# Audio tower, first attention: projections, turned blocks and output projection placed inside and behind the first pass

## What is computed

```python
h = _L0_tok_ref(x, L0_tok_W, L0_tok_b)
h = h + _L0_attn_ref(_layernorm(h, axis=-1), L0_attn_Wq, L0_attn_Wk, L0_attn_Wv, L0_attn_Wo, L0_attn_bo)
h = h + _L0_ffn_ref(_layernorm(h, axis=-1), L0_ffn_gate_w, L0_ffn_gate_b, L0_ffn_w1, L0_ffn_b1, L0_ffn_w2, L0_ffn_b2)
...
attn = jnp.einsum('bhqd,bhkd->bhqk', q, k)
causal_mask = jnp.triu(jnp.ones((T, T), dtype=bool), k=1)
attn = jnp.where(causal_mask, -jnp.inf, attn)
attn = jax.nn.softmax(attn, axis=-1)
out = jnp.einsum('bhqk,bhkd->bhqd', attn, v)
```

## Time and profile before

| what | value |
|---|---|
| median of 3 runs | 817.16 us (812.59 to 818.09) |
| the profiled execution's own time | 813.25 us |
| its span, first to last instruction | 811.4 us |
| mean granted TensorE clock | 0.948 of 2.4 GHz |
| TensorE busy | 715.2 us, 88% |
| VectorE busy | 446.1 us, 55% |
| ScalarE busy | 353.0 us, 44% |

### The profile page before, as it was taken

The page is one execution under the profiler, slowest core; times in us unless marked ns, Lnnn a source line. Parts: engine busy times, 40 slices in busy tenths (PEclk is TensorE's granted clock), DMA queues, the critical chain, the costliest instruction groups (busy, mean ns, idle before and its releaser), DMA issues.

```text
span 811.4 us, 16105 instructions
## 1 busy us (share of the span) xinstructions
PE 715.2 (88%) x5664; PEld 581.6 (72%) x5664; DVE 446.1 (55%) x1117; ACT 353.0 (44%) x602; POOL 137.8 (17%) x174
## 2 busy tenths in 40 slices
PE   6587998898898999999999999998899999998732
PEld 4466677676676999999999999996566665664411
DVE  4546766766655443244322232232768888866685
ACT  2242353253253322112222122222998998988351
POOL 2010111311311221000000100101552323211013
PEclk9799999999999999999999999999999999999755
DMA  6979474474365665655555655571874447650002
GB/s 178 210 97 246 55 92 66 66 91 69 55 86 182 220 216 176 240 188 190 160 182 189 211 194 159 194 195 46 111 116 76 72 64 105 79 70 9 1 26 78
DMA packets 70711, 102.67 MB, mean 127 GB/s; under 512 B 8160, under 2 KB 58472, under 8 KB 70512
## 3 DMA queue, kind: packets, MB, share of 16 engines
q1 hardware_dynamic: 67504, 93.34, 51.2%
q0 software_dynamic: 3136, 8.40, 4.1%
HBM read 63.88 MB, written 12.58 MB: 94 GB/s over the span
## 4 chain that ended last, share of the span: by engine, by line
PE 62%; DVE 17%; ACT 7%; issue 5%; DMA 5%; POOL 2%; SPq 1%; POOLq 0%; DVEq 0%; ACTq 0%
PE psum L1936 17%; PE psum L1987 17%; DVE arena L1285 8%; PE psum L1640 4%; DVE arena L1151 4%; PE psum L1648 3%; DMA arena<-arena 3%; PE psum L1879 3%; PE psum L1885 2%; PE psum L1703 2%; PE psum L1894 2%; PE psum L1682 1%; ACT arena L836 1%; ACT arena L835 1%; PE psum L1665 1%
## 5 line engine op out<-in xcount | busy, mean ns | idle before, releaser
L1936 PEld LDWEIGHTS psum<-arena 128*128 128x128 f32 x1248 | 144.9, 192 | 2.1 <-issue 0.2
L1936 PE MATMUL psum<-arena 128*128 128x128 f32 x1248 | 146.1, 275 | 0.1
L1987 PE MATMUL psum<-arena 128*128 x624 | 141.4, 380 | 1.2 <-DVE arena L1431 0.8
L865 ACT ACTIVATE arena<-psum,arena 128x128 f32<-128x128 f32 x156 | 44.5, 368 | 191.8 <-PE psum L1936 113.4
L1987 PEld LDWEIGHTS psum<-arena 128*128 128x128 f32 x624 | 115.5, 190 | 15.9 <-issue 1.8
L1413 DVE TENSOR_SCALAR arena<-psum,arena 128x128 f32<-128x128 f32 x156 | 43.9, 344 | 81.7 <-PE psum L1936 63.5
L1894 PE MATMUL psum<-arena 96*128 96x256 bf16 x512 | 75.8, 276 | 10.1 <-ACT arena L835 6.1
L1285 DVE TENSOR_TENSOR arena<-arena 128x1024 f32<-128x1024 f32 x64 | 80.0, 1316 | 4.9 <-ACT arena L835 2.6
L1894 PEld LDWEIGHTS psum<-arena 96*128 96x128 bf16 x512 | 45.0, 98 | 45.5 <-ACT arena L836 14.3
L702 POOL DMA_INDIRECT w0T<-yg,pos x32 | 37.4, 1169 | 223.2 <-DMA yg<-arena 176.8
L1431 DVE TENSOR_TENSOR arena<-psum,arena 128x256 f32<-128x256 f32 x39 | 16.6, 425 | 96.6 <-PE psum L1987 96.6
(11 more groups left out here) (288 smaller groups left out, 1192.9 us busy)
## 6 DMA issues: line engine op xcount, KB each, us to landing
arena<-in_L_ffn_w_dram SPq DMA_DIRECT2D x47, 1024.0 KB, 11.5
arena<-arena SPq DMA_DIRECT2D x192, 128.0 KB, 5.9
arena<-xg SPq DMA_DIRECT2D x39, 128.0 KB
yg<-arena SPq DMA_DIRECT2D x39, 128.0 KB, 1.7
out_dram<-arena SPq DMA_DIRECT2D x8, 256.0 KB, 2.1
xg<-zeros SPq DMA_DIRECT2D x9, 128.0 KB, 2.6
arena<-in_x_dram SPq DMA_DIRECT2D x8, 128.0 KB, 7.2
arena<-in_L_ffn_b_dram SPq DMA_DIRECT2D x1, 1024.0 KB, 12.2
```

What stands on the lines that cost most here:

```text
L865: ins = act.activation(hidT[:, v, c, :], psum[:, 2 * v, c * P:(c + 1) * P], ACT.Relu, bias=b1c[:, v, c:c + 1])
L1936: mm = pe.matmul(psum[:, 2 * v + c // HALF, (c % HALF) * P:(c % HALF + 1) * P], w1b[:, i % W1_BUFS, d, c * P:(c + 1) * P], xtT[:, v, d, :] ...
L1987: mm = pe.matmul(y_bank, hidT[:, u, c, :], w2s[:, one(e), c, :].rearrange("p o n -> p (o n)"), start=(c == 0), stop=(c == HC - 1))
```

## The change

No arithmetic changes; the order and two places do.

- The first pass uses two areas (banks 0 to 3), each pair waiting for the reduce two pairs back. Banks 4 and 5 are free during it.
- TensorE makes single pairs by `maxima(p)`. The next batch's input is turned behind pair 0, the router's input behind 1, the attention's last output behind 2; the router's logits (now in bank 6) stand behind pair 4, the k projection behind 5. Behind pair 7 follow the turned normalised output, q, the turned maxima (now in bank 4), the output projection and v; then the second pass, with nothing of the output projection in it.
- VectorE's reciprocals stand behind its third reduce, the gate logits and the normalised output behind its sixth. Behind the maxima it takes k's remainder, then q's. The residual add and statistics of batch b-1 come ahead of the token add of batch b+2, q's last part behind that, both normalisations ahead of the ranks.
- ScalarE sends the row of maxima on its own queue and casts k's high half first, during the first pass. The middle parts are cast ahead of the copy of v.
- SyncE sends k's parts ahead of q's and no longer waits for the maxima.
- The small products of the expert plan move from bank 7 to bank 6.

The core of the diff (what is only moved away in TensorE's program is in the listing above; `weights(p)` calls `shifted_scores`, `values(g)` calls `weigh_values`, `turned_input` is the turn behind `xh_done`):

```diff
         area = [psum[:, 0:2, :], psum[:, 2:4, :]]
-        area3 = [*area, psum[:, 4:6, :]]
...
-        early_cand = psum[:, 7, P:P + EARLY_TILES]
...
+        early_cand = psum[:, 6, P:P + EARLY_TILES]
+        turned_max = psum[:, 4, :].bitcast(BF16)
...
-                        sp.wait_ge(S["mT_done"], b + 1)
-                        sp.dma_start(stackq[SHIFT_ROW:SHIFT_ROW + 1, u], mT[0:HEADS, :]).then_inc(S["mrow"], 16)
                     if stages(b + 1, 0, LAST):
                         v = 1 - u
+                        spread(b + 1, v, 0, 1, S["kh_done"], S["stk_k"])
...
-                        spread(b + 1, v, 0, 1, S["kh_done"], S["stk_k"])
+                        spread(b + 1, v, 1, 1, S["km_done"], S["stk_k"])
                         spread(b + 1, v, 1, 0, S["qm_done"], S["stk_q"])
-                        spread(b + 1, v, 1, 1, S["km_done"], S["stk_k"])
+                        spread(b + 1, v, 2, 1, S["kl_done"], S["stk_k"])
                         spread(b + 1, v, 2, 0, S["ql_done"], S["stk_q"])
-                        spread(b + 1, v, 2, 1, S["kl_done"], S["stk_k"])
 
                 batches(sp, iteration, B)
...
                         act.copy(x2T.rearrange("p c t -> p (c t)"), misc[0]).then_inc(S["xt2_done"], 1)
+                    if stages(b + 1, 0, LAST):
+                        act.wait_ge(S["k_mm"], b + 2)
+                        wait(act, S["stk_k"], 16 * SLOTS6 * (b + 1))
+                        act.copy(qkp[1][:, 0].rearrange("p c t -> p (c t)"), misc[1]).then_inc(S["kh_done"], 1)
+                    if stages(b - 1, 0, LAST):
+                        act.wait_ge(S["ot2_mm"], b)
+                        wait(act, S["wo_mm"], b - 1)
+                        act.copy(oT.rearrange("p c t -> p (c t)"), turned[:, 1, :]).then_inc(S["oT_done"], 1)
                     if stages(b, 0, LAST):
                         act.wait_ge(S["mT_mm"], b + 1)
                         wait(act, S["mrow"], 16 * b)
-                        act.copy(mT[0:HEADS, :], misc[0].bitcast(BF16)[0:HEADS, 0:T]).then_inc(S["mT_done"], 1)
+                        act.copy(mT[0:HEADS, :], turned_max[0:HEADS, 0:T]).then_inc(S["mT_done"], 1)
+                        act.wait_ge(S["mT_done"], b + 1)
+                        act.dma_start(stackq[SHIFT_ROW:SHIFT_ROW + 1, u], mT[0:HEADS, :]).then_inc(S["mrow"], 16)
...
+                        act.wait_ge(S["kr_done"], b + 2)
+                        act.copy(qkp[1][:, 1], qkr[1]).then_inc(S["km_done"], 1)
+                        act.wait_ge(S["qr_done"], b + 2)
+                        act.copy(qkp[0][:, 1], qkr[0]).then_inc(S["qm_done"], 1)
...
+                    def maxima(p):
+                        if stages(b, 0, LAST):
+                            if p == 0:
+                                wait(dve, S["mneg_done"], 2 * b)
+                            dve.wait_ge(S["sn_mm"], PAIRS * b + p + 1)
+                            dve.tensor_reduce(mx[:, 2 * p:2 * p + 2, :],
+                                              area[p % 2][:, :, 0:3 * P].rearrange("p i (n k) -> p i n k", k=P),
+                                              AX, ALU.max).then_inc(S["mx_done"], 1)
+
                     if isinstance(b, int) and b == 0:
                         candidates()
+                    for p in range(3):
+                        maxima(p)
+                    if stages(b - 1, 0, LAST):
+                        dve.wait_ge(S["ot1_mm"], b)
+                        wait(dve, S["on_done"], QT * (b - 1))
+                        for q in range(QT):
+                            dve.reciprocal(rr[:, q, :], o1[:, q, :, DH]).then_inc(S["rr_done"], 1)
+                    for p in range(3, 6):
+                        maxima(p)
+                    if stages(b - 2, 0, LAST):
+                        gate_logits(b - 2, misc[0])
+                    if stages(b - 1, 0, LAST):
+                        wait(dve, S["ot2_mm"], b - 1)
+                        for q in range(QT):
+                            dve.wait_ge(S["rr_done"], QT * (b - 1) + q + 1)
...
+                    for p in range(6, PAIRS):
+                        maxima(p)
...
+                    if stages(b + 1, 0, LAST):
+                        wait(dve, S["km_done"], b + 1)
+                        wait(dve, S["kl_done"], b + 1)
+                        split_rest(b + 1, 1, S["kh_done"], S["kr_done"])
+                        wait(dve, S["qm_done"], b + 1)
+                        wait(dve, S["ql_done"], b + 1)
+                        split_rest(b + 1, 0, S["qh_done"], S["qr_done"])
...
-                        split_last(b + 1, 0, S["qm_done"], S["ql_done"])
                         split_last(b + 1, 1, S["km_done"], S["kl_done"])
+                    if stages(b - 1, 0, LAST):
+                        dve.wait_ge(S["wo_mm"], b)
+                        dve.wait_ge(S["hbo_done"], b)
+                        v = h[:, bass.ds((b - 1) * QT, QT), :]
+                        dve.tensor_tensor(v, misc[1].rearrange("p (q d) -> p q d", q=QT), v, ALU.add).then_inc(S["h1_done"], 1)
+                        dve.wait_ge(S["h1_done"], b)
+                        wait(dve, S["xn_done"], QT * (b - 1))
+                        statistics(b - 1, 1, S["stat2"], S["mv2"])
...
+                def scores_for_max(b, u, p):
...
+                    if p < 2:
+                        wait(pe, S["exp_done"], PAIRS * b - 1 + p)
+                    else:
+                        pe.wait_ge(S["mx_done"], PAIRS * b + p - 1)
+                    for i in range(2):
+                        hd = 2 * p + i
+                        dst = area[p % 2][:, i, :]
...
+                    maxima(0)
+                    if not (isinstance(b, int) and b == 0):
+                        turned_input()
+                    maxima(1)
                     if stages(b - 2, 0, LAST):
...
                         turn(misc[0], lambda q, c: x2h[:, u, q, c * P:(c + 1) * P], S["xt2_mm"])
+                    maxima(2)
                     if stages(b - 1, 0, LAST):
                         pe.wait_ge(S["oa_done"], b)
...
+                    maxima(3)
+                    maxima(4)
+                    if stages(b - 2, 0, LAST):
+                        pe.wait_ge(S["xt2_done"], b - 1)
...
+                        mm.then_inc(S["lg_mm"], 1)
+                    maxima(5)
+                    if stages(b + 1, 0, LAST):
+                        pe.wait_ge(S["xT_done"], b + 2)
...
+                        project_rows(misc[1], 1, S["k_mm"])
+                    maxima(6)
+                    maxima(7)
+                    if stages(b - 1, 0, LAST):
+                        pe.wait_ge(S["on_done"], QT * b)
+                        turn(turned[:, 1, :], lambda q, c: onat[:, q, c * P:(c + 1) * P], S["ot2_mm"])
+                    if stages(b + 1, 0, LAST):
+                        wait(pe, S["gl_done"], b - 1)
+                        project_rows(misc[0], 0, S["q_mm"])
...
                     if stages(b, 0, LAST):
...
                         for q in range(QT):
-                            mm = pe.transpose(misc[0].bitcast(BF16)[0:HEADS, q * P:(q + 1) * P], mneg[:, q, :], identb[:])
+                            mm = pe.transpose(turned_max[0:HEADS, q * P:(q + 1) * P], mneg[:, q, :], identb[:])
                         mm.then_inc(S["mT_mm"], 1)
...
+                    if stages(b - 1, 0, LAST):
+                        pe.wait_ge(S["oT_done"], b)
+                        upto(pe, "kr_done", b + 1)
+                        project_tokens(misc[1], oT, lambda c: w0T[:, 3, c, :], S["wo_mm"])
                     if stages(b + 1, 0, LAST):
...
                         wait(pe, S["mT_done"], b + 1)
...
                         project_tokens(turned[:, 0, :], xT, lambda c: w0T[:, 2, c, :], S["v_mm"])
...
                     if stages(b, 0, LAST):
                         pe.wait_ge(S["mrow"], 16 * (b + 1))
-                        shifted_scores(b, u, 0)
-                        shifted_scores(b, u, 1)
+                    weights(0)
+                    weights(1)
```

204 lines of the change are left out of this document (78 added, 126 removed).

## The result

The changed kernel takes 794.06 us (median of 4 runs, 793.29 to 795.36) beside 817.09 for the kernel before (812.59 to 818.09) on the same chip: a ratio of 0.973, interval 0.969 to 0.977. It is 23 us faster, against 32 forecast (817 to 785); the time lies inside the range. Between the two profiled executions the spans fell from 811.4 to 793.6 us, 17.8 less against 29.6 forecast.

What follows compares the result with a forecast made beforehand. No engine was taken as full: they take turns in eight attention rounds. Shorter rounds, VectorE last, total 202.8 against 232.4 us; 813.25 less 29.6 is 783.7, with drift 785, range 776 to 799.

Steps and rivals of the forecast that it cites:

- The full round, 26.3: Rounds 4 to 7: VectorE's 20.9 busy, 1.9 small gaps, 2.1 before reduces and 1.4 new wait; gain 3.5 on 29.8 us.
- the new wait: VectorE, between k's remainder and q's, waits for ScalarE's cast of q's high half behind the row's issue: 1.4 us.
- The first pass, forecast at about 10: Score products and reduces with TensorE's moved work inside: about 10 us for TensorE and VectorE, against 9.6 before.
- VectorE is the last: In a full round VectorE's 26.3 us outlasts TensorE's 25.6 and the transfers' 24.4 to 25, so it sets the length.
- The third chain: Stack transfers of q and k: complete 24.4 to 25 us into a full round, under 1.5 to spare, the next bound.
- The 2.1 before reduces: VectorE's waits before first-pass reduces, 2.1 us a round, kept because a reduce started late beside GpSimd's add.
- The sum of 25.1 a round: Full-round length if, by the port rule, a reduce reading only PSUM does not stand still: 25.1 us.
- Two areas, 0.3 a round: First pass: each pair waits for the reduce two back, costing 0 to 1.5 us a round, taken as 0.3.
- Round 2, 24.5: Second round: 24.3 us by the 3.5 gain; transfers behind four weight megabytes make it 24.5, against 27.8 before.
- the rival I called slower: Row of maxima lands only with stack transfers, 11.6 us; 7.0 in each of eight rounds, time 840; chance 0.04.
- the forecast of the last round, 23.5: Round 8, without next projections: output projection's 1.9 and 0.6 of order go, 23.5 us against 26.0 before.
- 202.8 forecast: All eight rounds of the first attention together: 202.8 us against 232.4 before, 29.6 less.

Runs made afterwards that it cites:

- eleventh experiment: Changed kernel with round 2's weights later, eight unread last-round products, q's last part earlier, and scaling and first scan filling VectorE's wait for q: 793.7 us, ratio 0.971.
- fourth: Changed kernel with q's last part made on VectorE right behind k's last part, ahead of both additions and their statistics: 793.8 us, ratio 0.970.
- fifth: Changed kernel with the output projection back in the second pass and the earlier order of additions, norms and ranks: 795.6 us beside 804.7, ratio 0.987.
- sixth: Changed kernel with k's projection directly ahead of q's, behind the first pass's last pair, instead of between pairs 5 and 6: 793.6 us beside 804.7, ratio 0.987.
- last experiment: Changed kernel with GpSimd's four scatters held until the last reduce of the first pass: 797.2 us, ratio 0.978.
- third experiment: Kernel before with two bank areas instead of three in the first pass, nothing else changed: 813.8 us, ratio 0.997.
- the one execution that stands in for the changed kernel: Changed kernel with GpSimd's output-bias addition cut from 2x256 to 2x8 columns, other columns' bias left out, executed once: 784.3 us beside 804.7.
- tenth: Changed kernel with round 2's 4 MB of expert weights behind its stack transfers and eight unread products added in the last round: 790.9 us, ratio 0.971.
- seventh experiment: Kernel before with only the row of maxima sent by ScalarE instead of SyncE: 804.6 us, ratio 0.998.

## Why the prediction was right, and where it was too good

**The full round, 26.3: right in its length.** Measured 26.7 and 26.5 at full clock on this chip. Its terms: VectorE busy 20.7 to 20.9 (20.9 forecast), the new wait 1.6 to 1.8 (1.4), the waits before reduces and the reciprocal 0.50 + 0.41 + 1.04 + 0.54 = 2.5 (2.1 for reduces). TensorE is busy 24.7, not 25.6. The first pass, forecast at about 10, takes 10.8 from the first reduce to the end of the last (140.06 to 150.84), and the second pass, forecast at about 9.2, 9.8 (155.64 to 165.39). Round 3, 25.6 forecast for want of scatters, took 25.3.

**"VectorE is the last": only half right.** The third chain, of which I had written that it was the next bound, runs beside it. Filling VectorE's wait for q (eleventh experiment) and making q's last part earlier (fourth) bought nothing. What did move the next start is an earlier cast of q's high half: by 1.1 us with the row from SyncE, for a round shorter by 0.9, and by 1.2 on the second chip, where the reduces have no gaps (12.8 us up to the cast and 12.4 behind it, 13.96 and 12.49 in the changed kernel). Rounds 4 to 6 of the kernels with the changed order (the fifth and sixth experiments aside, which alter it) take 12.3 to 12.9 from there, except the last, which takes 13.4 to 13.6 as VectorE holds TensorE up. In these 12 us TensorE and the transfers are full together; no run parts the two. So VectorE counts up to the cast, where it alternates with TensorE, and behind it only once it is late, as in the last experiment.

**Where the gain came from.** At the same clock of 1.00 on this chip a round 4 with two areas alone (third experiment) is 12.6 up to the cast and 16.3 behind it, the changed kernel's 14.0 and 12.7. So the first part did not get shorter but longer, by 1.3, and the second shorter by 3.5, as TensorE's work there fell from 15.6 to 12.1 us: k's projection and two turns of blocks now stand ahead of the cast, while the output projection stays behind it for the most part, at another place. By the experiments k's place is worth about 2.0 us a full round and the output projection's 1.0 with the cover that it gives the row, both against the one execution that stands in for the changed kernel. These do not add up to the whole, as each fills waits that the other leaves.

**The 2.1 before reduces: right size, wrong cause.** I read the gap of 1.21 beside GpSimd's addition as held by it, against the Trainium skill's rule that the prediction cites. The addition stands beside reduces with 0.18 of gap, or none, in the kernels with k beside q and with the row alone moved. The reduces beside it agree with the Trainium skill ("SBUF — State Buffer", Who interferes with whom), by which a reduce of PSUM is not held by the port it shares with GpSimd. The gaps belong to the rounds with scatters and leave the pass with them. The sum of 25.1 a round that I had worked out by that rule is near what the second chip shows, 25.2, in part by luck, since VectorE's chain alone does not set the round.

**Two areas, 0.3 a round: nothing in the kernel before.** The ratio there is 0.997 (0.994 to 1.001); in the changed kernel, where products stand between the pairs, it was not measured by itself.

**Round 2, 24.5: mis-sized, 29.1.** I had counted the 4 MB of weights against the stack transfers and not against the row of maxima. It is the mechanism of the rival I called slower, in one round of eight: the row landed in 6.5 us with the weights under way, free only up to about 3.4, and TensorE stood 3.1; the clock of 0.50 for 3 us behind that wait is the rest. With the weights sent later the round took 25.0, at 1.00. The Trainium skill ("DMA: Bandwidth & Descriptors", Queues, rings and completion order) had said it, for any queue: a row on ScalarE's ring (2.2, at most 6.5) and on SyncE's (2.3, at most 7.6) landed alike here. In the other rounds the rival stayed away, as k's transfers were nearly done: with k sent just ahead the median landing is 4.3 and TensorE waits 11.2 us in all.

**The clock: the term that I left out.** I took 1.00 for every round. Round 6 had 0.94 and took 28.0, against 26.5 for its neighbour with the same work: TensorE busy 26.26 against 24.71. Round 8 had 0.81. In the profiles with the changed order one of rounds 4 to 6 is low in some (round 6 here, round 4 with the weights later), several in two (the row from SyncE and the eleventh experiment), and none in others, the changed kernel run again among them; in the kernel before seven of eight rounds are, rounds 4 to 7 at 0.94. So part of the gain is also the clock's: a full round of before takes 30.5, 29.8 and 30.5 at 0.94, but 28.9 at 1.00 with two areas alone, which cost nothing. Against 28.9 the change is worth 2.2 to 2.5 us a full round, not the 3.5 forecast; the rest is the low clock of those rounds in the profile before. And the forecast of the last round, 23.5, was too short even without a low clock: 24.6, 24.6 and 25.4 in three profiles at 1.00 (fourth, eleventh and tenth experiments, the last two with eight added products). In the result's round 8 VectorE waits 3.8 us for the output projection, which comes at half clock; it waits 2.0 in those three.

**The sum.** 202.8 forecast and 213.8 measured: 4.6 in round 2, 1.7 in round 6, 3.8 in round 8, 0.8 in round 1, 0.1 in the rest.

## What to carry to other kernels

Work is worth moving from a stretch in which its engine is full into one in which it waits: here 3.5 us came off the second and 1.3 were added to the first. Split the round at the instruction between the two, compare both parts at the same clock, and see how far each engine is from being the last behind it before filling waits there. A small DMA that the path waits for is put against all traffic of its moment, weights for later included, not only against its own queue. And a sum of a long alternating pass needs a term for the clock, read from how many rounds of the kernel before show a low one.

## What the runs showed of the hardware

- On two of the three chips VectorE stood still for 0.4, 1.0 and 0.5 us in a first pass beside GpSimd's four indirect DMAs, with the products long in place (the pair's last product at 143.34 or 143.63, the reduce at 144.63 in the changed kernel); on the third the same code had at most 0.2. Holding the scatters removed them. They are a part of the 12 us between the kernel before on two of these chips (817 and 805); another may be the clock, low in seven rounds in the profile on the first and in four on the second, with the row alone moved. What differs between the chips, and what in a scatter holds VectorE, stays open.
- A VectorE subtraction with two SBUF inputs took 1.6 us longer beside GpSimd's addition of two SBUF inputs, in each of three rounds (last experiment), while reduces of PSUM beside the same addition had at most 0.2 us of gap. The Trainium skill ("SBUF — State Buffer", Who interferes with whom) says both; the trace agrees. By the profile, whose times on GpSimd are rough, VectorE had begun 0.4 us before the addition each time and was the one that lost.
- The low clock is not fixed to a place: of two profiles of the changed kernel one has it in round 6 and the other in no round from 3 to 7. It is also not all of the spread: the same kernel ran in 789.8 us at a mean clock of 0.959 and in 797.6 at 0.956 on one chip; with the weights later in 787.4 at 0.964 and 794.8 at 0.949. TensorE had been idle for most of 2 us ahead of the stretch of 10 us at 0.50 in the last round; but with 0.60 busy of 2 us in another profile's last round it stayed at 1.00, and with 0.44 it stayed once (the row from SyncE) and fell once (the weights later), so no rule is read from this.
- A row of 8 KB on ScalarE's queue costs 0.51 to 0.61 us of issue and lands in 1.8 at the least; put alone into the kernel before (seventh experiment), the middle of eight is 1.8 too, as from SyncE's queue.
